# Attention over 32 heads: the sums of the values rotate through one line of four PSUM banks, and their matmuls come in pairs behind every four scores

## The chip, the cores and the metric

The kernel runs on one core of one Trainium2 chip. Its time is the device time of one execution in microseconds (us). A core has a TensorE (PE in the rows; its weight loads are PEld), a VectorE (DVE), a ScalarE (ACT), a GpSimd (POOL) and a SyncE (SP), each with its own instruction stream. They tell each other of progress by semaphores only. PSUM, where TensorE writes, has eight banks of 128 partitions x 512 fp32; this stage of the kernel uses all eight.

## The reference, cut to what matters

Two blocks, each attention or state-space plus feed-forward, behind a LayerNorm with modulation. The change lies in the first attention alone. It has N=2 batches, S=1024 tokens, D=128 and 16 heads of 8 columns, so 32 (batch, head) pairs:

```python
q = (x @ Wq.T).reshape(N, S, H, hd).transpose(0, 2, 1, 3)      # k, v likewise
energy = jnp.einsum('nhqd,nhkd->nhqk', q, k)
attn = jax.nn.softmax(energy / jnp.sqrt(jnp.float32(hd)), axis=3)
out = jnp.einsum('nhql,nhld->nhqd', attn, v)
```

The softmax's maximum is taken off for each query, so the kernel computes every score twice: once to find the row's maximum, once for the exponential.

## The kernel before, in words

**Legs.** The stage is 16 legs (`NLEG`). A leg is four heads and one half (512) of their queries. For one leg the engines do this:

- `pe_max_score`, called "m": 32 matmuls of 512 columns with 48 rows of the array, bf16 (the fp32 numbers are split in three bf16 parts). Two of them fill one pair of the four `max_ps` banks, that is one tile. `ve_max_score` reduces a tile of 1024 to a maximum per query on VectorE, 16 tiles a leg. The first matmul of a tile waits until the tile two before it has been reduced.
- `pe_score`, called "s": 32 matmuls of 512 columns with 51 rows; the last three rows carry the maximum. Each fills one PSUM bank, which `ac_exp` on ScalarE turns into a 128 x 512 piece of `exp_scores`. The 51 rows of a score and the 48 rows of a maximum lie in different halves of the array for neighbours in the order, so the two run side by side.
- `pe_av`, called "v": the values' sum. One call is four matmuls (the records show eight, since fp32 goes in two passes), each on 32 of the 128 columns of the array and all 128 rows, for 256 queries. 16 calls make a leg; all add into one bank. `ac_av_out` on ScalarE then copies that bank to `av_t`, the mark by which legs are counted below.
- `results`: four fp32 transposes of `av_t` into a bank (`pe_out`), copied to `av_tok` by ScalarE; VectorE's reciprocal and POOL's product follow. `max_turn`: one transpose of the leg's maxima (`pe_max_turn`), copied by ScalarE and sent to the rows of `q_rows` by SP.

**Order.** Everything is issued by one loop over 4 * 16 + 1 rounds. The string `ROUNDS[n % 4]` gives the order of the letters m, s and v in a round: 8 m, 8 s, 4 v. The scores of round n are those of leg n // 4, the maxima run 22 tiles ahead, and the values one round behind, so a leg's first value call stands in the second round of the leg. TensorE, ScalarE and VectorE each run their list in this order, and an instruction that waits holds all behind it on its engine. The maxima of the last leg are done some 40 us before the stage ends; from there on the m's of the string issue nothing.

**Banks.** Before the change the scores, the turn of the maxima and the turn of the results share three banks (`score_k`) in strict rotation: the u-th user takes bank u % 3 and waits until the user u - 3 has been read. The values' sum has a bank of its own (`av_ps`). The first value call of a leg therefore waits for `ac_av_out` of the leg before. To give ScalarE time for that, the string of the second round has four pairs "ms" ahead of its first v, behind two that end the round before.

**Memory for the exponentials.** `exp_scores` has four buffers; the first exponential of a group waits for the value calls of the group four before, which were issued long ago in either order.

Of the kernel before, what the change touches and what calls it, by code (L numbers as in the profile page):

```python
# [3 lines left out]

# [2 lines left out]

# [5 lines left out]
F32 = mybir.dt.float32  # L15
# [7 lines left out]
P = 128  # L23
# [6 lines left out]
CH = 512  # L30
# [96 lines left out]
def wait_from(engine, sem, n):  # L127

    if n > 0:
        engine.wait_ge(sem, n)  # L130
# [16 lines left out]
class Kernel:  # L147
# [294 lines left out]
    def attention(self):  # L442
        nc, A, pe, ve, ac, po, sp = self.nc, self.A, self.pe, self.ve, self.ac, self.po, self.sp
        with ExitStack() as scope:
# [21 lines left out]
            back = [sb(f"av_tok{s}", [P, CH]) for s in range(2)]  # L466
            rows_set, v_set = self.sig("rows_set"), self.sig("v_cols_set")
            mps = scope.enter_context(nc.psum_tensor("max_ps", [P, 4, CH], F32))
            eps = scope.enter_context(nc.psum_tensor("score_k", [P, 3, CH], F32))
            avp = scope.enter_context(nc.psum_tensor("av_ps", [P, CH], F32))  # L470

# [57 lines left out]


            NLEG, NU, AHEAD = BH // 2, 16, 22
            read = []

            def score_bank():

                u = len(read)
                return u % 3, read[u - 3] if u > 2 else (exped.sem, 0)

            def head_rows(leg, j):

# [102 lines left out]
            def max_turn(leg):  # L645

                bank, free = score_bank()
                pe_max_turn(leg, bank, free)
                ac_max_turn(leg, bank)
                sp_max_turn(leg)  # L650
                read.append(turn_read.at())

            def results(leg):

                bank, free = score_bank()
                pe_out(leg, bank, free)
                ac_out(leg, bank)
                read.append(res_out.at())

            def divide(leg):  # L660
                ve_recip(leg)
# [27 lines left out]
            def score(e):  # L689
                if e < 32 * NLEG:  # L690
                    bank, free = score_bank()
                    pe_score(e // 32, e % 32, bank, free)
                    ac_exp(e // 32, e % 32, bank)
                    read.append(exped.at())

            def pe_av(leg, kt, half):


                a, quad = 8 * leg + kt, leg // 2
                qs = slice(half * CH // 2, (half + 1) * CH // 2)  # L700
                if kt == half == 0:
                    pe.wait_ge(v_put.sem, 4 * quad + 4)
                    wait_from(pe, av_out.sem, leg)
                pe.wait_ge(exped.sem, 4 * a + 4)
                for j in range(4):
                    mm = pe.matmul(avp[32 * j:32 * j + 32, qs], va[quad % 2][:, j, kt, :], pt[a % 4][:, j, qs],  # L706
                                   start=(kt == half == 0), stop=(kt == TB - 1), skip_group_check=True)
                if half:
                    mm.then_inc(*av_mm.up())

            def ac_av_out(leg):
                ac.wait_ge(av_mm.sem, 8 * leg + 8)
                wait_from(ac, out_mm.sem, leg - 1)
                ac.activation(ot[leg % 2][:], avp[:], ACT.Copy).then_inc(*av_out.up())

            def ve_gate_heads(b, k):
                ve.tensor_tensor(
# [9 lines left out]


            ring = self.ring
            ring.bind([eps[:, k, :] for k in range(3)] + [avp[:]], first=4)  # L730
            self.ac_silu_c(0)
            cols_ps = self.pe_mod_cols(0)
            ac.wait_ge(*self.in_k.at())
# [154 lines left out]
            def ve_first_batch(step):  # L888


                two = range(step % 4 * 2, step % 4 * 2 + 2)
                if step == 0:
                    ve.wait_ge(divided.sem, NLEG // 2)
                    ve.wait_ge(*m_row0)
                if 0 <= step < 4:
                    for k in two:
                        ve_gate_heads(0, k)
                if step == 4:
                    ve_add_heads(0, TB)
                    ve.wait_ge(*gated.at())  # L900
                if 4 <= step < 8:
                    for t in two:
                        self.ve_ln_stat(self.X, t)
                if step == 8:
                    self.ve_ln_aggr(0, TB)
                    roots.append(self.po_ln_root(0, TB))
                if 12 <= step < 16:
                    normed.extend(self.ve_ln_apply(self.X, t, roots[0]) for t in two)
# [17 lines left out]

            ROUNDS = ("msmsvmsmsvvmsmsvmsms", "msmsmsmsvmsmsvvmsmsv", "msmsvmsmsvmsmsvmsmsv", "msmsvmsmsvmsmsvmsmsv")
            normed, roots = [], []  # L930
            for n in range(4 * NLEG + 1):
                leg, place = n // 4, n % 4
                e, v, a = 8 * n, 2 * AHEAD + 8 * n, 4 * n - 4
                for what in ROUNDS[place]:
                    if what == "s":
                        score(e)
                        e += 1
                    elif what == "m":
                        max_score(v)
                        v += 1  # L940
                        if v % 2 == 0:
                            ve_first_batch(v // 2 - NLEG * NU - 1)
                    elif n:
                        pe_av(a // 16, a // 2 % 8, a % 2)
                        if a % 16 == 15:
                            ac_av_out(a // 16)
                        a += 1
                if place == 0 and leg:
                    if leg % 2 == 0 and leg < NLEG:
                        po_put_v(leg // 2)  # L950
                if place == 1 and 0 < leg < NLEG:
                    results(leg - 1)
                if place == 2 and 0 < leg < NLEG:
                    divide(leg - 1)
                    if leg == NLEG - 1:
# [2166 lines left out]
```

## Time and profile before

| | us |
|---|---|
| median of 3 runs (lowest, highest) | 1151.91 (1146.47, 1158.07) |
| the profiled execution | 1158.34 |
| its span, first to last instruction | 1157.0 |
| TensorE busy in the span | 1040.8 (90%) |
| VectorE busy | 974.8 (84%) |
| ScalarE busy | 805.0 (70%) |
| TensorE's mean granted clock | 0.935 |

The attention stage of the change lies between 62 us, when the first exponential starts, and 391 us. In the page's 40 slices of 29 us these are slices 3 to 13. The busy share of TensorE counts matmuls from issue to the modelled end of a record, and neighbours overlap; 99% is therefore no proof that the array is full. In the timeline a matmul's row says when it starts; how fast matmuls can follow one another is read from the distance of starts.

The granted clock is 1.00 at 2.4 GHz and 0.50 at 1.2 GHz.

### The profile page before, as it was taken

To read this page: it belongs to the slowest core of one execution; us is meant where nothing else is said; L and a number is where in the kernel's file an instruction comes from. 1 tells how busy PE (TensorE), PEld (TensorE's weight loads), DVE (VectorE), ACT (ScalarE), POOL (GpSimd) and SP (SyncE) were. 2 spreads that over 40 slices of the span, in tenths; PEclk is the share of its full clock that TensorE was granted. 3 is DMA by queue.
4 is the path that set the end of the run, shared out by engine and by line. 5 is a ranking of instruction groups with operands and counts; after the bars stand their busy time and mean duration, and the time that the engine had idled before them with its cause. 6 is when DMAs were issued, how large, how long until landed. Compare 5 with 4: busy or idle time off the path is not lost. (4 is left out here: it accounts for less than half of the span.)

```text
span 1157.0 us, 21250 instructions
## 1 busy us (share of the span) xinstructions
PE 1040.8 (90%) x7771; PEld 648.1 (56%) x7771; DVE 974.8 (84%) x1319; ACT 805.0 (70%) x1576; POOL 539.3 (47%) x485
## 2 busy tenths in 40 slices
PE   6899999999999887898999999899999994699994
PEld 4222222222222233357998885468888873398883
DVE  6889999999995577879999997889999997787774
ACT  3279988999997553896988862998888832255551
POOL 5400431010101112015988993038999983168884
PEclk9779999999997798889999999899999996699998
DMA  5210100001004330015999990108999976443335
GB/s 156 68 43 15 30 15 19 26 16 30 15 2 74 93 76 16 6 55 123 248 242 230 219 245 6 59 8 193 228 250 231 231 173 241 86 93 64 63 63 135
DMA packets 65608, 121.17 MB, mean 105 GB/s; under 512 B 15598, under 2 KB 33902, under 8 KB 65504
## 3 DMA queue, kind: packets, MB, share of 16 engines
q0 software_dynamic: 19872, 52.79, 24.5%
q1 hardware_dynamic: 43928, 64.82, 18.0%
q10 hardware_dynamic: 1704, 2.20, 0.6%
q8 instruction: 63, 1.03, 0.4%
q14 instruction: 41, 0.34, 0.1%
HBM read 58.02 MB, written 13.32 MB: 62 GB/s over the span
## 5 line engine op out<-in xcount | busy, mean ns | idle before, releaser
L2258 PEld LDWEIGHTS m_pair<-filter_w,delta_x_t 128*128 128x128 f32 x2560 | 294.0, 192 | 42.3 <-issue 42.3
L571 DVE TENSOR_REDUCE neg_max<-max_ps 128x1 f32<-128x1024 f32 x256 | 295.8, 1214 | 16.5 <-PE max_ps L560 16.2
L2258 PE MATMUL m_pair<-filter_w,delta_x_t 128*128 128x112 f32 (+3 forms) x2560 | 298.5, 276 | 9.1 <-DVE h_t L2285 3.3
L687 ACT ACTIVATE exp_scores<-score_k 128x512 f32<-128x512 f32 x512 | 271.1, 606 | 37.0 <-PE score_k L679 31.5
L2234 ACT ACTIVATE decay<-delta,a_log 128x1024 f32<-128x1024 f32 x128 | 145.7, 1142 | 49.2 <-DVE normed L2285 29.2
L560 PE MATMUL max_ps<-k_rows,q_rows 48*128 48x512 bf16 x512 | 163.4, 401 | 12.4 <-DVE neg_max L571 10.7
L679 PE MATMUL score_k<-q_rows,k_rows 51*128 51x512 bf16 x512 | 167.5, 399 | 2.4 <-ACT exp_scores L687 0.6
L2226 ACT ACTIVATE filter_w<-filter,b_t 128x112 f32<-128x112 f32 (+1 forms) x576 | 167.4, 374 | 0.0
L706 PE MATMUL av_ps<-exp_scores,v_cols 128*32 128x256 f32 x2048 | 163.6, 405 | 0.0
L580 POOL CAST neg_max_parts<-neg_max 128x16 bf16<-128x16 f32 x16 | 3.1, 196 | 236.6 <-DVE neg_max L571 236.6
L706 PEld LDWEIGHTS av_ps<-exp_scores,v_cols 128*32 128x32 f32 x2048 | 44.9, 110 | 97.3 <-ACT exp_scores L687 50.0
L560 PEld LDWEIGHTS max_ps<-k_rows,q_rows 48*128 48x128 bf16 x512 | 29.5, 95 | 117.2 <-DVE neg_max L571 75.5
L2276 DVE TENSOR_TENSOR_SCAN m_pair<-decay,m_pair 128x1024 f32<-128x1024 f32 x38 | 87.0, 2290 | 1.6 <-PE m_pair L2258 1.2
L2323 POOL TENSOR_TENSOR h_t<-h_t,c_row 128x1024 f32<-128x1024 f32 x30 | 81.4, 2715 | 12.1 <-DVE h_t L2285 12.1
L2323 POOL TENSOR_TENSOR normed<-normed,c_row 128x1024 f32<-128x1024 f32 x28 | 76.0, 2715 | 23.7 <-DVE normed L2285 23.7
L2285 DVE TENSOR_TENSOR_SCAN normed<-decay,m_pair 128x1024 f32<-128x1024 f32 x32 | 73.0, 2281 | 8.8 <-PE m_pair L2258 8.8
L2285 DVE TENSOR_TENSOR_SCAN h_t<-decay,m_pair 128x1024 f32<-128x1024 f32 x32 | 73.0, 2281 | 6.0 <-PE m_pair L2258 6.0
L2929 PE MATMUL gate_up_ps<-tile_t,gate_up 128*128 128x128 f32 x624 | 76.3, 275 | 0.0
L2929 PEld LDWEIGHTS gate_up_ps<-tile_t,gate_up 128*128 128x128 f32 x624 | 72.6, 192 | 0.0
L2973 POOL DMA_INDIRECT moe_sum<-tile_out,row_to x39 | 62.1, 1592 | 20.5 <-issue 10.7
L2371 PE MATMUL m_pair<-delta_x,ident 128*128 128x512 f32 x136 | 68.3, 598 | 0.0
L2942 ACT ACTIVATE silu_gate<-gate 128x512 f32<-128x512 f32 x39 | 24.6, 631 | 59.1 <-DVE gate L2937 59.1
(330 smaller groups left out, 1611.2 us busy)
## 6 DMA issues: line engine op xcount, KB each, us to landing
c_row<-c_rows SPq DMA_DIRECT2D x64, 512.0 KB, 6.0
x_inner<-normed POOLq DMA_DIRECT2D x16, 512.0 KB, 6.7
delta_x<-mod_memory POOLq DMA_DIRECT2D x15, 512.0 KB, 8.2
delta_x<-x_inner POOLq DMA_DIRECT2D x15, 512.0 KB, 8.2
x_inner<-h_t POOLq DMA_DIRECT2D x14, 512.0 KB, 6.1
mod_memory<-h_t POOLq DMA_DIRECT2D x14, 512.0 KB, 9.3
mod_memory<-normed POOLq DMA_DIRECT2D x12, 512.0 KB, 9.1
gate_up_all<-in_gate_up_w SPq DMA_DIRECT2D x8, 512.0 KB, 7.1
```

The costliest lines, as they stand in the source:

```text
L560: mm = pe.matmul(mps[:, t % 2 * 2 + half, :], qp[row:row + KR, s, leg % 2, qt * P:(qt + 1) * P], kp[row:row + KR, s, half * CH:(half + 1) ...
L571: ve.tensor_reduce(nm[leg % 2][:, 4 * j + qt:4 * j + qt + 1], mps[:, bank:bank + 2, :].rearrange("p a q -> p (a q)"), AX_X, ALU.max, negat ...
L679: pe.matmul(eps[:, bank, :], kp[row:row + KM, s, kt * P:(kt + 1) * P], qp[row:row + KM, s, leg % 2, :], start=True, stop=True).then_inc(*s ...
L687: ac.activation(pt[a % 4][:, HEADS[r % 4], :], eps[:, bank, :], ACT.Exp, scale=SC).then_inc(*exped.up())
L706: mm = pe.matmul(avp[32 * j:32 * j + 32, qs], va[quad % 2][:, j, kt, :], pt[a % 4][:, j, qs], start=(kt == half == 0), stop=(kt == TB - 1) ...
L2226: w = ac.activation(wf[g % 3][:, lo:c * STEP + P], tri[min(c, 1)][:], ACT.Copy, scale=self.bT[b][:, c, n:n + 1])
L2234: ac.activation(da[u % 4], delta[:, blk, b, :], ACT.Exp, scale=am[:, l, blk, n:n + 1]).then_inc(*decay.up())
L2258: mm = pe.matmul(vps[blk][:, lo:hi], self.duT[b][:, c, blk * P:(blk + 1) * P], wf[g % 3][:, lo:hi], start=True, stop=True)
L2276: ve.tensor_tensor_scan(to, da[u % 4], vps[0][:], 0.0, ALU.mult, ALU.add).then_inc(*hs.up())
L2285: ve.tensor_tensor_scan(hh[g % 4], da[u % 4], vps[1][:], 0.0, ALU.mult, ALU.add).then_inc(*hs.up())
L2323: po.tensor_tensor(yacc[b][1] if n == 1 else hh[g % 4], hh[g % 4], csb[g % 3][:], ALU.mult).then_inc(*yg.up())
L2929: mm = pe.matmul(gups[j % 2][:, half, f * P:(f + 1) * P], gu[j % 3][:, half * FF + f * P:half * FF + (f + 1) * P], xt[j % 2][:], start=Tru ...
```

## The change

The private bank of the values goes away. Four banks of `score_k` stand in one line (`idle_banks`): who needs a bank takes the first in the line, and it goes to the end of the line, with the semaphore that tells when it was read. The first value call of a leg takes the first bank of the line and keeps it until `ac_av_out`, so the scores have three banks while a leg's values are summed, as before, and four from the issue of `ac_av_out` to the next leg's first value call.

The strings of `ROUNDS` are new. Every half round is four pairs "ms" and then two v. `results` moves from the end of the second round of a leg to a place inside it (the letter "o", behind its fifth pair).

```diff
-            eps = scope.enter_context(nc.psum_tensor("score_k", [P, 3, CH], F32))
-            avp = scope.enter_context(nc.psum_tensor("av_ps", [P, CH], F32))
+            eps = scope.enter_context(nc.psum_tensor("score_k", [P, 4, CH], F32))
...
-            read = []
+            idle_banks = deque((k, (exped.sem, 0)) for k in range(4))
+            av_bank = {}
             def score_bank():
-                u = len(read)
-                return u % 3, read[u - 3] if u > 2 else (exped.sem, 0)
+                return idle_banks.popleft()
...
-                    read.append(exped.at())
+                    idle_banks.append((bank, exped.at()))
...
                 if kt == half == 0:
+                    av_bank[leg], free = score_bank()
                     pe.wait_ge(v_put.sem, 4 * quad + 4)
-                    wait_from(pe, av_out.sem, leg)
+                    wait_from(pe, *free)
...
-                ac.activation(ot[leg % 2][:], avp[:], ACT.Copy).then_inc(*av_out.up())
+                ac.activation(ot[leg % 2][:], eps[:, av_bank[leg], :], ACT.Copy).then_inc(*av_out.up())
+                idle_banks.append((av_bank[leg], av_out.at()))
...
-            ROUNDS = ("msmsvmsmsvvmsmsvmsms", "msmsmsmsvmsmsvvmsmsv", "msmsvmsmsvmsmsvmsmsv", "msmsvmsmsvmsmsvmsmsv")
+            ROUNDS = ("msmsmsmsvvmsmsmsmsvv", "msmsmsmsvvmsomsmsmsvv", "msmsmsmsvvmsmsmsmsvv", "msmsmsmsvvmsmsmsmsvv")
...
+                    elif what == "o":
+                        if 0 < leg < NLEG:
+                            results(leg - 1)
...
-                if place == 1 and 0 < leg < NLEG:
-                    results(leg - 1)
```

How the list of TensorE changes is seen at three places. The names: L560 (L559 after the change) is m, L679 (L678) is s, L706 is v, L622 (L621) the turn of the results; `exped` counts the exponentials done, `max_read` the reduced tiles.

TensorE in the middle of a leg, before:

```order
L706 MATMUL av_ps<-exp_scores,v_cols 32x256 x3
L560 MATMUL max_ps<-k_rows,q_rows 128x512 [waits max_read]
L679 MATMUL score_k<-q_rows,k_rows 128x512 [waits exped]
L560 MATMUL max_ps<-k_rows,q_rows 128x512
L679 MATMUL score_k<-q_rows,k_rows 128x512 [waits exped]
L706 MATMUL av_ps<-exp_scores,v_cols 32x256 [waits exped]
L706 MATMUL av_ps<-exp_scores,v_cols 32x256 x3
```

and after the change, from one pair of value calls to the next:

```order
L706 MATMUL score_k<-exp_scores,v_cols 32x256 x3
L559 MATMUL max_ps<-k_rows,q_rows 128x512 [waits max_read]
L678 MATMUL score_k<-q_rows,k_rows 128x512 [waits exped]
L559 MATMUL max_ps<-k_rows,q_rows 128x512
L678 MATMUL score_k<-q_rows,k_rows 128x512 [waits exped]
L559 MATMUL max_ps<-k_rows,q_rows 128x512 [waits max_read]
L678 MATMUL score_k<-q_rows,k_rows 128x512 [waits exped]
L559 MATMUL max_ps<-k_rows,q_rows 128x512
L678 MATMUL score_k<-q_rows,k_rows 128x512 [waits exped]
L706 MATMUL score_k<-exp_scores,v_cols 32x256 [waits exped]
L706 MATMUL score_k<-exp_scores,v_cols 32x256 x3
L706 MATMUL score_k<-exp_scores,v_cols 32x256 [waits exped]
```

Between two stretches of value matmuls there stand four scores in place of two, and the stretch is two calls long. A leg has 8 such stretches in place of 14.

TensorE where the values of a new leg begin, before (two more pairs, and the last value call of the old leg, stand ahead of these rows):

```order
L560 MATMUL max_ps<-k_rows,q_rows 128x512
L679 MATMUL score_k<-q_rows,k_rows 128x512 [waits exped]
L560 MATMUL max_ps<-k_rows,q_rows 128x512 [waits max_read]
L679 MATMUL score_k<-q_rows,k_rows 128x512 [waits exped]
L560 MATMUL max_ps<-k_rows,q_rows 128x512
L679 MATMUL score_k<-q_rows,k_rows 128x512 [waits exped]
L706 MATMUL av_ps<-exp_scores,v_cols 32x256 [waits exped,av_out,v_put]
L706 MATMUL av_ps<-exp_scores,v_cols 32x256 x3
```

and after:

```order
L706 MATMUL score_k<-exp_scores,v_cols 32x256 x3
L559 MATMUL max_ps<-k_rows,q_rows 128x512 [waits max_read]
L678 MATMUL score_k<-q_rows,k_rows 128x512 [waits exped]
L559 MATMUL max_ps<-k_rows,q_rows 128x512
L678 MATMUL score_k<-q_rows,k_rows 128x512 [waits exped]
L559 MATMUL max_ps<-k_rows,q_rows 128x512 [waits max_read]
L678 MATMUL score_k<-q_rows,k_rows 128x512 [waits exped]
L559 MATMUL max_ps<-k_rows,q_rows 128x512
L678 MATMUL score_k<-q_rows,k_rows 128x512 [waits av_out]
L706 MATMUL score_k<-exp_scores,v_cols 32x256 [waits exped,v_put]
L706 MATMUL score_k<-exp_scores,v_cols 32x256 x3
```

The six pairs without a value call have become four, as anywhere else. The wait for `av_out` has moved from the value call to the fourth score, which gets the bank of the old sum.

TensorE at the turn of the results, after (before, L622 stood between two stretches, right behind a value call):

```order
L559 MATMUL max_ps<-k_rows,q_rows 128x512 [waits max_read]
L678 MATMUL score_k<-q_rows,k_rows 128x512 [waits exped]
L621 MATMUL score_k<-ident,av_t 128x128 [waits exped,av_out]
L621 MATMUL score_k<-ident,av_t 128x128 x3
L559 MATMUL max_ps<-k_rows,q_rows 128x512
L678 MATMUL score_k<-q_rows,k_rows 128x512 [waits exped]
L559 MATMUL max_ps<-k_rows,q_rows 128x512 [waits max_read]
L678 MATMUL score_k<-q_rows,k_rows 128x512 [waits exped]
L559 MATMUL max_ps<-k_rows,q_rows 128x512
L678 MATMUL score_k<-q_rows,k_rows 128x512 [waits res_out]
L706 MATMUL score_k<-exp_scores,v_cols 32x256 [waits exped]
```

The turn now takes one of the three banks in the midst of four scores: the third waits for the exponential of the first, the fourth for the copy of the results (`res_out`).

## Rows read from the trace of the kernel before

**Rows 1.** Windows of two legs: length, busy PE, PEld, DVE, ACT, POOL, granted clock, DMA, GB/s.

```profile
206.26:225.72 19.46, 19.11 (x201) 5.58 (x197) 18.50 (x18) 17.92 (x36) 1.95 (x9) 1.00 0.07 22
...
166.07:186.76 20.69, 19.18 (x201) 5.57 (x197) 19.64 (x28) 17.92 (x37) 5.29 (x14) 1.00 0.07 21
```

**Rows 2.** The page's costliest groups: operation, count | busy us, mean ns | idle before, releaser.

```profile
L571 DVE TENSOR_REDUCE neg_max<-max_ps 128x1 f32<-128x1024 f32 x256 | 295.8, 1214 | 16.5 <-PE max_ps L560 16.2
...
L687 ACT ACTIVATE exp_scores<-score_k 128x512 f32<-128x512 f32 x512 | 271.1, 606 | 37.0 <-PE score_k L679 31.5
```

**Rows 3.** Timeline of ACT, marks of legs: start us, us, engine, line, out<-in, count.

```profile
86.96 0.60 ACT L714 ACTIVATE av_t<-av_ps 128x512 f32<-128x512 f32 x1
...
361.90 0.60 ACT L714 ACTIVATE av_t<-av_ps 128x512 f32<-128x512 f32 x1
...
389.37 0.60 ACT L714 ACTIVATE av_t<-av_ps 128x512 f32<-128x512 f32 x1 [2.41 <-PE av_ps L706]
```

**Rows 4.** Timeline of PE and ACT between value groups.

```profile
227.85 0.39 PE L679 MATMUL score_k<-q_rows,k_rows 51*128 51x512 bf16 x1
...
228.17 0.64 PE L706 MATMUL av_ps<-exp_scores,v_cols 128*32 128x256 f32 x8
...
229.27 1.07 PE L706 MATMUL av_ps<-exp_scores,v_cols 128*32 128x256 f32 x16
...
230.28 0.39 PE L679 MATMUL score_k<-q_rows,k_rows 51*128 51x512 bf16 x1
...
230.71 1.08 ACT L687 ACTIVATE exp_scores<-score_k 128x512 f32<-128x512 f32 x2 [0.39 <-PE score_k L679]
```

**Rows 5.** Timeline of ACT and PE: an exponential, and the score that waited for it.

```profile
226.20 0.62 ACT L687 ACTIVATE exp_scores<-score_k 128x512 f32<-128x512 f32 x1
...
226.87 0.39 PE L679 MATMUL score_k<-q_rows,k_rows 51*128 51x512 bf16 x1
```

**Rows 6.** Timeline of PE: turns of results and of maxima, each with the next score.

```profile
231.38 0.66 PE L622 MATMUL score_k<-ident,av_t 128*128 128x128 f32 x4
...
231.97 0.39 PE L679 MATMUL score_k<-q_rows,k_rows 51*128 51x512 bf16 x1
...
236.40 0.24 PE L602 MATMUL score_k<-identb,neg_max_parts 128*48 128x128 bf16 x1
...
236.57 0.39 PE L679 MATMUL score_k<-q_rows,k_rows 51*128 51x512 bf16 x1
```

**Rows 7.** Timeline of PE where the last leg's values begin, and its last values.

```profile
360.98 0.64 PE L706 MATMUL av_ps<-exp_scores,v_cols 128*32 128x256 f32 x8
361.55 0.91 PE L679 MATMUL score_k<-q_rows,k_rows 51*128 51x512 bf16 x3
...
364.56 1.08 PE L706 MATMUL av_ps<-exp_scores,v_cols 128*32 128x256 f32 x8
...
386.20 3.10 PE L706 MATMUL av_ps<-exp_scores,v_cols 128*32 128x256 f32 x40
```

**Rows 8.** Windows (columns of rows 1) with the granted clock, end of the stage and first leg.

```profile
358.00:363.80 5.80, 5.10 (x43) 1.37 (x41) 2.14 (x8) 5.21 (x11) 1.47 (x1) 1.00 1.14 210
363.90:387.60 23.70, 23.60 (x130) 5.19 (x133) 5.38 (x26) 13.00 (x25) 1.62 (x3) 0.50 0.21 34
...
62.00:73.70 11.70, 11.14 (x63) 2.31 (x58) 9.23 (x8) 8.48 (x16) 0.00 (x0) 0.50 0.19 57
```

**Rows 9.** Timeline of PE and ACT in the first leg, at the low clock.

```profile
69.91 1.94 PE L706 MATMUL av_ps<-exp_scores,v_cols 128*32 128x256 f32 x16
...
71.78 0.61 PE L679 MATMUL score_k<-q_rows,k_rows 51*128 51x512 bf16 x1
...
72.18 0.63 PE L679 MATMUL score_k<-q_rows,k_rows 51*128 51x512 bf16 x1
...
72.43 1.08 ACT L687 ACTIVATE exp_scores<-score_k 128x512 f32<-128x512 f32 x2 [1.75 <-PE score_k L679]
...
72.74 1.08 PE L706 MATMUL av_ps<-exp_scores,v_cols 128*32 128x256 f32 x8
```

More of the change, by code:

```diff
@@ L7 @@
-from collections import namedtuple
+from collections import deque, namedtuple
 from contextlib import ExitStack
@@ L650, in max_turn @@
                 sp_max_turn(leg)
-                read.append(turn_read.at())
+                idle_banks.append((bank, turn_read.at()))
             def results(leg):
@@ L657, in results @@
                 ac_out(leg, bank)
-                read.append(res_out.at())
+                idle_banks.append((bank, res_out.at()))
             def divide(leg):
@@ L701, in pe_av @@
                 if kt == half == 0:
+                    av_bank[leg], free = score_bank()
                     pe.wait_ge(v_put.sem, 4 * quad + 4)
-                    wait_from(pe, av_out.sem, leg)
+                    wait_from(pe, *free)
                 pe.wait_ge(exped.sem, 4 * a + 4)
                 for j in range(4):
-                    mm = pe.matmul(avp[32 * j:32 * j + 32, qs], va[quad % 2][:, j, kt, :], pt[a % 4][:, j, qs],
+                    mm = pe.matmul(eps[32 * j:32 * j + 32, av_bank[leg], qs], va[quad % 2][:, j, kt, :], pt[a % 4][:, j, qs],
                                    start=(kt == half == 0), stop=(kt == TB - 1), skip_group_check=True)
@@ L729, in attention @@
             ring = self.ring
-            ring.bind([eps[:, k, :] for k in range(3)] + [avp[:]], first=4)
+            ring.bind([eps[:, k, :] for k in range(4)], first=4)
             self.ac_silu_c(0)
```

## The prediction

> **What bounds the stage now.** I first read the windows of whole legs [rows 1]. A leg in mid stage takes 19.46 us. VectorE is busy in 18.50 of them and ScalarE in 17.92, so both are nearly full and neither is quite the bound. In the page's groups VectorE's 16.5 us of idle time ahead of the reductions is almost all put down to TensorE, and so are 31.5 us of ScalarE's ahead of the exponentials [rows 2]: TensorE's list, in which one waiting instruction holds all others, deals the time out. The marks of the legs [rows 3] give 361.90 - 86.96 = 274.94 us for 14 legs. Twelve of 19.46 and two of 20.69 make 274.9; the two long ones carry 1.14 us more of VectorE's work [rows 1]. The last leg, which has no maxima left and so should be shorter, took 27.47 us.
>
> Why it did is in the windows with the clock [rows 8]. Up to 363.8 us the granted clock is 1.00, from 363.9 to 387.6 it is 0.50, the 1.2 GHz level. The timeline [rows 7] shows what TensorE did before it fell: a value call at 360.98, then six lone scores, three of them late behind ScalarE, and the next value call only at 364.56. It rose again at the end, where the last value calls stand back to back [rows 7]. The change moves both things, the mid leg and the last leg, and in opposite directions.
>
> **Mid leg, the time of a half round after the change.** It is four pairs "ms" and two value calls. Three banks are left to the scores while a leg's values are summed, so the fourth score waits until the exponential of the first is done. This gives a closed chain, and every link of it has a row:
>
> - first score to the start of its exponential: 230.28 to 230.71, 0.43 us [rows 4];
> - the exponential: 0.60 [rows 2];
> - its end to the score that waits for the bank: 226.82 to 226.87, 0.05 [rows 5];
> - the fourth score to the first value call: 227.85 to 228.17, 0.32 [rows 4];
> - a pair of value calls to the next first score: 229.27 to 230.28, 1.01 [rows 4].
>
> The sum is 2.41 us. VectorE needs 18.50 / 8 = 2.31 for its two tiles of it and hides under this; the first matmul of the second tile starts before the fourth score and waits for nothing longer. Before the change the same bank count did little harm: only two scores stood between value calls, so the third bank's exponential ran under the values.
>
> Three of a leg's eight half rounds are others. With the turn of the results in it, the fourth score waits for that turn's copy. The turn starts 0.32 behind the first score, its records last 0.66 [rows 6], and then come 0.05, a copy of 0.60 and 0.05: 1.68 in place of 0.43 + 0.60 + 0.05 = 1.08, so 3.0. The turn of the maxima adds 236.40 to 236.57, 0.17 [rows 6]: 2.6. At the change of leg the fourth score waits for `av_t`: the pair's 1.07 [rows 4], 0.05, 0.60 and 0.05, then 0.32, which is 2.1; the first exponential queues behind `av_t`, so I take 2.25. A leg is 5 x 2.41 + 3.0 + 2.6 + 2.25 = 19.9 us, **0.44 more than before**. Its lower bound is VectorE's 18.5; above it I allow 20.2, if the reductions come late as well. The two long legs I leave at 20.7: VectorE's extra work has 19.9 - 18.5 = 1.4 of slack to hide in, but the maxima wait for it in the same list. Sum for the mid stage: 12 x 0.44 = **+5.3 us** (bounds -13 and +10).
>
> What the change takes away on TensorE does not show in this: a value stretch costs 0.32 less the 0.21 that 512 columns take at 2.4 GHz on the way in, and 1.01 less two calls of 0.43 (1.07 - 0.64, or 0.43, from the two forms in [rows 4]) on the way out, 0.26 together. Six stretches fewer are 1.5 us of TensorE a leg. They fall into the wait of the fourth score. The Trainium skill, "TensorEngine Tiling (Array Packing)", Key Properties, says that changing the tiling mode drains the engine. The rows agree that a change costs time, and by this rule alone each leg would get shorter by the drains saved.
>
> **Last leg.** From `av_t` of leg 14 there are six half rounds with scores: 2.25, 3.0 and four of 2.41, or 14.9. Two pairs of value calls follow, 0.86 each, so 16.6 us at the full clock against 27.47: **-10.8 us**. It needs the clock to stay up. The reason to think so: no stretch between value calls is now longer than four scores, where the clock fell behind six; and in mid leg, with the same spacing as in the second half of the stage, the trace has 1.00 throughout [rows 1]. If the clock falls nevertheless, the gain is near 1 (below). The bounds are -11 and 0.
>
> **First leg.** Until 73.7 us the clock is 0.50 [rows 8], in both kernels. Values begin at the same place. I take 0, with bounds of -1.5 (the clock rises a little earlier, since a pair stands at the very start) and +3 (later).
>
> **Other edits.** Ahead of the stage the banks of the projections rotate as before, the same four under other names: 0. On the other engines VectorE's, POOL's and SP's lists are unchanged, and ScalarE issues the same instructions with the results' copy a few places earlier: its work of 17.92 a leg stays under 19.9. The reciprocal and the product get their input earlier, and nobody waits for them in mid stage. The first value call no longer waits for `av_t`; the fourth score ahead of it does, already counted.
>
> **Sum.** On the profiled execution, 1158.34 + 5.3 - 10.8 = 1152.8. That execution lies 6.4 above the median shown, 1151.91. The lowest run, 1146.47, is 11.9 below it, about what a low-clock last leg costs; if some runs before keep the clock there, the median already holds part of my gain, while the cost in mid leg stays. Against the median the two terms nearly cancel. I predict **1153 us**, with 1148 to 1158 as this case's own range. About 1% (11.5 us) is what a measurement of this kernel tells from no change: below 1140.4 is faster, above 1163.4 slower.
>
> **Rivals.**
>
> - *The last leg runs at the low clock all the same.* At 1.2 GHz a half round is 71.78 to 72.43, 0.65, then 0.60 and 0.05, 72.18 to 72.74, 0.56, and 69.91 to 71.78, 1.87 [rows 9]: 3.7 us. The last leg is then 6 x 3.7 + 0.6 + 0.3 for its two odd ones and 2 x 1.73, some 26.5, and the total 1158.34 + 5.3 - 1.0 = 1162.6. For it: the scores fill less than half the rows of the array, and TensorE waits for a bank in every half round. Against it: the shorter stretches without values. Chance 0.15.
> - *The drains were the bound.* If the fourth score's wait is hidden, VectorE sets the leg: 18.5. Then 14 legs save 0.96 each, 13.4, and with the last leg the total is 1158.34 - 13.4 - 10.8 = 1134. For it: TensorE is named for VectorE's idle time, and it has 1.5 us less to do. Against it: the chain of 2.41, none of whose links the change shortens. By the rule of the Trainium skill's page "TensorEngine Tiling (Array Packing)" on drains this would be the time. Chance 0.10.
> - *The clock falls or stays down elsewhere, and it is slower.* The place is the first leg. The clock rose at 73.7 behind value calls that stood close [rows 9]; if the even order with its wait on the fourth score does not bring it up, a leg costs 8 x 3.7 + 1 = 30.6 in place of 19.9. One leg more at the low clock makes 1153 + 10.7 = 1163.7, which is the point from which it decides; with the last leg low as well it is 1173. Against it: each leg of before kept 1.00 once it had it, through six pairs without values. The Trainium skill, "TensorE: Matmul & The Clock Gate", A second HAM failure mode, reports a kernel whose clock swung because TensorE idled briefly between groups as it cycled through PSUM banks; the trace has such waits in each leg at a steady 1.00, so it speaks against the rule so far. Chance 0.08.
> - *The order does not matter*, as the three score banks were not waited for and the clock is a matter of luck: 1152. Chance 0.07, and it falls within my range.
>
> My forecast has 0.60. **Faster** gets 0.13: the drains, and a little of the forecast where median runs keep the clock better than I think. **Slower** gets 0.13: the clock, and that part of the low last leg that ends above 1163.4. **Same** gets 0.74. The range of 1141 to 1164 takes in the low last leg and part of the way to the faster case; outside lie most of the drains' case and the clock's.
>
> **What would show it.** Marks of `av_t` 19.9 us apart in mid stage, value calls in pairs 2.4 us apart with one gap of 3.0 and one of 2.6 a leg, each pair behind a score that waited for ScalarE; VectorE idle 1.4 us a leg, not 0.96. The last leg at 1.00 and near 16.6 us. Marks 18.5 apart would refute the chain. A last leg above 25 us with a clock of 0.50 would refute the second term.

## The result, and the profile after

The changed kernel takes 1161.04 us (median of 11 runs, 1156.13 to 1163.76) against 1148.35 us of the kernel before (11 runs beside it, 1143.78 to 1158.07). The ratio is 1.0102 with a 95% interval of 1.0075 to 1.0129: 1% slower. The forecast was 1153 with a range of 1141 to 1164 and most of the chance on "within 1%"; the time lies in the range, 8.0 us above the forecast, and the ratio just beyond the 1% that parted "same" from "slower" there. Ratios leave out executions far above the rest (one of 1854.45 us with single value calls and the line, one of 1947.98 us of the kernel before); the medians and counts given below have them in. The profiled execution of the changed kernel took 1158.43 us, almost the same as the 1158.34 of the profile before. That agreement is the sum of two large differences, and another execution of the kernel before lacks most of the second (the last experiment).

The windows of the changed kernel answer to those of before [rows 1, 8]. The columns are the same: a mid leg, one of the two long legs, the last leg, and the 14 legs from the first to the fifteenth `av_t`.

```profile
231.41:251.66 20.25, 19.92 (x199) 6.55 (x197) 18.94 (x18) 17.80 (x36) 1.24 (x5) 1.00 0.08 21
127.42:149.03 21.61, 19.68 (x199) 6.47 (x197) 20.20 (x28) 17.90 (x36) 4.05 (x12) 1.00 0.06 20
373.18:390.03 16.85, 14.24 (x157) 5.91 (x156) 5.39 (x26) 13.40 (x26) 1.62 (x3) 1.00 0.32 52
86.90:373.18 286.28, 276.08 (x2739) 91.36 (x2736) 264.08 (x282) 249.42 (x491) 44.60 (x124) 1.00 0.08 22
```

A mid leg is 20.25 us, 0.8 longer; a long leg 21.61, 0.9 longer; 14 legs are 286.28 in place of 274.94, **11.3 us longer**. The last leg is 16.85 at a clock of 1.00, where it was 27.47 [rows 3, 8]: **10.6 us shorter**. The first `av_t` stands at 86.90, before at 86.96, and from the last one to the end of the span it is 767.1 us, before 767.6. With these two small differences the two large ones add up to the 0.1 us that lie between the profiles.

The page's groups of the stage:

```profile
L686 ACT ACTIVATE exp_scores<-score_k 128x512 f32<-128x512 f32 x512 | 266.1, 604 | 43.6 <-PE score_k L678 39.8
...
L678 PE MATMUL score_k<-q_rows,k_rows 51*128 51x512 bf16 x512 | 169.2, 391 | 6.3 <-ACT exp_scores L686 4.6
```

and the scores' row in that of before:

```profile
L679 PE MATMUL score_k<-q_rows,k_rows 51*128 51x512 bf16 x512 | 167.5, 399 | 2.4 <-ACT exp_scores L687 0.6
```

ScalarE's wait for scores has grown from 31.5 [rows 2] to 39.8 us, and that of the scores on TensorE for ScalarE from 0.6 to 4.6. In the view of waits of two legs (211 to 252 us) the loads of the scores' weights wait 5.2 us for the exponentials, where two legs of before (206 to 245 us) have 2.3:

```profile
PEld score_k L678 <- ACT exp_scores L686: 5.2, 12, 0.5
...
ACT exp_scores L686 <- PE score_k L678: 4.0, 10, 0.4
```

The loop shows in the timeline of TensorE from one pair of value calls to the next (every row of the score L678 and of the pair L706, the maxima left out):

```profile
246.60 0.39 PE L678 MATMUL score_k<-q_rows,k_rows 51*128 51x512 bf16 x1
...
246.83 0.38 PE L678 MATMUL score_k<-q_rows,k_rows 51*128 51x512 bf16 x1
...
247.19 0.39 PE L678 MATMUL score_k<-q_rows,k_rows 51*128 51x512 bf16 x1
...
247.74 0.39 PE L678 MATMUL score_k<-q_rows,k_rows 51*128 51x512 bf16 x1
248.06 1.07 PE L706 MATMUL score_k<-exp_scores,v_cols 128*32 128x256 f32 x16
...
249.07 0.39 PE L678 MATMUL score_k<-q_rows,k_rows 51*128 51x512 bf16 x1
```

and in that of ScalarE, the same stretch and the next leg's beginning:

```profile
247.09 2.06 ACT L686 ACTIVATE exp_scores<-score_k 128x512 f32<-128x512 f32 x4 [0.40 <-PE score_k L678]
249.55 2.07 ACT L686 ACTIVATE exp_scores<-score_k 128x512 f32<-128x512 f32 x4 [0.40 <-PE score_k L678]
251.66 0.60 ACT L714 ACTIVATE av_t<-score_k 128x512 f32<-128x512 f32 x1
252.15 2.78 ACT L686 ACTIVATE exp_scores<-score_k 128x512 f32<-128x512 f32 x5
254.86 0.60 ACT L628 ACTIVATE av_tok<-score_k 128x512 f32<-128x512 f32 x1
```

The first score starts at 246.60 and its exponential at 247.09, which ends 0.60 later; the fourth score starts at 247.74, 0.05 behind that end. (The third starts together with the maxima's matmul ahead of it, which waits for a reduction; the fourth comes later still, so this wait does not decide.) Then come the pair at 248.06 and the next first score at 249.07. ScalarE does four exponentials in 2.06 us and then is idle for 0.40, each time until the first score behind the pair.

### The profile page after: what moved, and what is told of

Same layout as the page of the kernel before. It is cut to its first block and busy times, and to the rows that moved or that the text cites. A ratio compares the mean times of both kernels' runs of the same rounds, so it can differ in the third digit from the quotient of the medians.

```text
span 1157.1 us, 21250 instructions
## 1 busy us (share of the span) xinstructions
PE 1039.2 (90%) x7771; PEld 661.5 (57%) x7771; DVE 979.9 (85%) x1319; ACT 802.6 (69%) x1576; POOL 538.8 (47%) x485
## 5 line engine op out<-in xcount | busy, mean ns | idle before, releaser
L570 DVE TENSOR_REDUCE neg_max<-max_ps 128x1 f32<-128x1024 f32 x256 | 300.5, 1220 | 21.6 <-PE max_ps L559 15.6
L686 ACT ACTIVATE exp_scores<-score_k 128x512 f32<-128x512 f32 x512 | 266.1, 604 | 43.6 <-PE score_k L678 39.8
L2236 ACT ACTIVATE decay<-delta,a_log 128x1024 f32<-128x1024 f32 x128 | 145.7, 1141 | 47.9 <-DVE normed L2287 27.9
L678 PE MATMUL score_k<-q_rows,k_rows 51*128 51x512 bf16 x512 | 169.2, 391 | 6.3 <-ACT exp_scores L686 4.6
L559 PE MATMUL max_ps<-k_rows,q_rows 48*128 48x512 bf16 x512 | 161.4, 403 | 10.4 <-DVE neg_max L570 7.5
L706 PE MATMUL score_k<-exp_scores,v_cols 128*32 128x256 f32 x2048 | 137.8, 387 | 1.6
L559 PEld LDWEIGHTS max_ps<-k_rows,q_rows 48*128 48x128 bf16 x512 | 30.5, 96 | 121.4 <-DVE neg_max L570 85.5
L706 PEld LDWEIGHTS score_k<-exp_scores,v_cols 128*32 128x32 f32 x2048 | 55.1, 109 | 54.6 <-issue 31.6
L678 PEld LDWEIGHTS score_k<-q_rows,k_rows 51*128 51x128 bf16 x512 | 38.7, 94 | 60.3 <-ACT exp_scores L686 47.8
L2975 POOL DMA_INDIRECT moe_sum<-tile_out,row_to x39 | 62.0, 1589 | 20.8 <-DVE tile_out L2965 10.5
```

What stands on the lines that cost most here:

```text
L559: mm = pe.matmul(mps[:, t % 2 * 2 + half, :], qp[row:row + KR, s, leg % 2, qt * P:(qt + 1) * P], kp[row:row + KR, s, half * CH:(half + 1) ...
L570: ve.tensor_reduce(nm[leg % 2][:, 4 * j + qt:4 * j + qt + 1], mps[:, bank:bank + 2, :].rearrange("p a q -> p (a q)"), AX_X, ALU.max, negat ...
L678: pe.matmul(eps[:, bank, :], kp[row:row + KM, s, kt * P:(kt + 1) * P], qp[row:row + KM, s, leg % 2, :], start=True, stop=True).then_inc(*s ...
L686: ac.activation(pt[a % 4][:, HEADS[r % 4], :], eps[:, bank, :], ACT.Exp, scale=SC).then_inc(*exped.up())
L706: mm = pe.matmul(eps[32 * j:32 * j + 32, av_bank[leg], qs], va[quad % 2][:, j, kt, :], pt[a % 4][:, j, qs], start=(kt == half == 0), stop= ...
L2236: ac.activation(da[u % 4], delta[:, blk, b, :], ACT.Exp, scale=am[:, l, blk, n:n + 1]).then_inc(*decay.up())
```

## The experiments

Each was profiled and timed against the kernel before. I name them by what they are; "leg" is the distance of two marks of `av_t` in mid stage, read from windows as above.

**The line of banks alone**, the order of before:

```diff
-            ROUNDS = ("msmsmsmsvvmsmsmsmsvv", "msmsmsmsvvmsomsmsmsvv", ...
+            ROUNDS = ("msmsvmsmsvvmsmsvmsms", "msmsmsmsvmsmsvvmsmsv", "msmsvmsmsvmsmsvmsmsv", "msmsvmsmsvmsmsvmsmsv")
...
-                    elif what == "o":
-                        if 0 < leg < NLEG:
-                            results(leg - 1)
...
+                if place == 1 and 0 < leg < NLEG:
+                    results(leg - 1)
```

> The one line of four banks alone, with the order of before (14 stretches of value calls a leg, the turn of the results at the end of the second round). Theory A (the time of a leg is the chain first score, exponential, fourth score, pair of value calls, so the order is what costs): the marks of av_t stay near 19.4 us apart, 1147 to 1149 us in all, ratio 0.998 to 1.003 to before. Theory B (the line costs, since scores now queue behind av_t's copy and the results): marks near 20.2, ratio near 1.01. The six lone scores of the last leg are still there, so its clock can fall to 0.50 as before.

```profile
225.23:244.56 19.33, 18.60 (x201) 5.53 (x197) 18.50 (x18) 17.85 (x37) 1.24 (x5) 1.00 0.08 22
...
360.51:378.88 18.37, 17.91 (x159) 5.52 (x158) 5.39 (x26) 14.55 (x29) 1.62 (x3) 0.91 0.43 64
```

The legs are 19.33 us, 0.13 shorter than before. The line is a small gain and not the loss. The ratio was 1.0056 (1.0022 to 1.0091) all the same, above the 1.003 that I had as the upper end, since the runs fall in two groups: five at 1145 to 1149, with a mean granted clock of 0.939 to 0.941, and five at 1156 to 1159, with 0.925 to 0.932. None of the upper group was profiled. In the profiled one, of the lower group, the clock was at 0.50 for a short while only, and the last leg took 18.37:

```profile
364.00:367.30 3.30, 3.30 (x27) 0.86 (x26) 0.00 (x0) 1.89 (x5) 0.00 (x0) 0.50 1.00 153
```

**The pairs alone**, with the private bank (the change's ROUNDS and its "o" in the kernel before):

> The new order (pairs of value calls behind four scores, results inside the second round) with the values' private bank and three rotating banks as before. Theory A: marks at least as far apart as in the changed kernel, 20.3 to 20.7 us, since the first value call of a leg now waits for av_t as well; ratio to before 1.010 to 1.016. Theory B (the line costs): marks near 19.5, ratio near 1.00.

```profile
232.88:253.41 20.53, 20.24 (x199) 6.48 (x197) 18.94 (x18) 17.81 (x35) 1.25 (x5) 1.00 0.08 21
```

20.53 us a leg, 1165.57 us, ratio 1.0171 (1.0127 to 1.0215). The order is the whole of the loss, and the line gives 0.27 a leg of it back. (The order is two things here, the pairs and the turn of the results inside a round; no run parts them.)

**Single value calls behind every two scores**, with the line:

```diff
-            ROUNDS = ("msmsmsmsvvmsmsmsmsvv", ...
+            ROUNDS = ("msmsvmsmsvmsmsvmsmsv",) * 4
...
-                    elif what == "o":
-                        if 0 < leg < NLEG:
-                            results(leg - 1)
...
+                if place == 1 and 0 < leg < NLEG:
+                    results(leg - 1)
```

> The line of four banks kept, but every round is four times (four m/s letters, one value call): single value calls behind every two scores, 16 stretches a leg. Theory A: the fourth score no longer follows the first one before a value stretch, so TensorE's wait for ScalarE hides under the value call and VectorE sets the leg: marks 18.7 to 19.0 us apart although TensorE changes tiling twice as often; about 0.6 us less than before on 14 legs, and the last leg near 15.6 us at clock 1.00: 1138 to 1143 us, ratio 0.990 to 0.994. Theory C (changes between value calls and scores are what TensorE pays for): two stretches a leg more than before cost 0.26 us each, marks near 20.0, ratio 1.005 to 1.01.

```profile
221.54:240.20 18.66, 18.66 (x201) 5.26 (x197) 18.32 (x18) 17.95 (x36) 1.24 (x5) 1.00 0.08 23
122.20:143.81 21.61, 20.01 (x199) 5.38 (x197) 20.41 (x28) 18.10 (x36) 4.98 (x13) 0.92 0.07 20
352.12:367.64 15.52, 15.52 (x157) 4.97 (x156) 5.39 (x26) 13.59 (x27) 1.62 (x3) 1.00 0.47 67
```

18.66 us a leg. 1137.49 us, ratio 0.9915 (0.9880 to 0.9950), faster than either kernel, with 16 stretches of value calls a leg, the most of all orders. Theory C, by which the changes between value calls and scores are what TensorE pays for, had asked for marks near 20.0; it falls as the account of the changed kernel.

What bounds this leg is not what I expected. VectorE is busy in 18.32 us of it and waits for TensorE once, for 0.34. TensorE's records leave no gap, and in the timeline its list runs at its own pace:

```profile
226.61 0.38 PE L678 MATMUL score_k<-q_rows,k_rows 51*128 51x512 bf16 x1
226.92 0.64 PE L706 MATMUL score_k<-exp_scores,v_cols 128*32 128x256 f32 x8
...
227.49 0.39 PE L678 MATMUL score_k<-q_rows,k_rows 51*128 51x512 bf16 x1
...
227.72 0.38 PE L678 MATMUL score_k<-q_rows,k_rows 51*128 51x512 bf16 x1
```

The distances of 0.31, 0.57 and 0.23 us make 1.11 for each stretch, 16 times a leg, and the two turns, at 0.59 and 0.24, and one wait of 0.13 fill the rest of the 18.66. So TensorE is full here and VectorE nearly so. With the 0.26 us a stretch that the prediction worked out, 16 switches are some 4.2 us of TensorE's list (an estimate); what they would give back in this order was not tried. The long legs did not gain: 21.61 us, with a mean clock of 0.92 in that window.

**The same order with the private bank:**

> The same even single value calls with the private bank and three rotating banks of before. Theory A: the first value call of a leg waits for av_t once, some 0.3 us a leg more than with the line: marks near 19.1, ratio 0.993 to 0.998. If the line has no part in it: marks as in the run with the line, 18.8.

19.00 us a leg, 1142.48 us, ratio 0.9959 (0.9932 to 0.9987). The line is worth 0.34 a leg here.

**Half an exponential** in the changed kernel; from the fifth group on, half of `exp_scores` keeps old values:

```diff
-                ac.activation(pt[a % 4][:, HEADS[r % 4], :], eps[:, bank, :], ACT.Exp, scale=SC).then_inc(*exped.up())
+                cols = slice(0, CH if a < 4 else CH // 2)
+                ac.activation(pt[a % 4][:, HEADS[r % 4], cols], eps[:, bank, cols], ACT.Exp, scale=SC).then_inc(*exped.up())
```

> The changed kernel, but from the fifth group of scores on the exponential covers only 256 of the 512 columns (the rest of exp_scores keeps old values): one link of the chain gets 0.2 us shorter. Theory A: a half round falls from 2.46 to about 2.3 us, where VectorE takes over, and marks from 20.26 to about 19.3. Theory D (the long stretch of two value calls starves VectorE's reductions): nothing of it changes, marks stay at 20.26.

```profile
226.73:245.92 19.19, 18.22 (x199) 6.43 (x197) 18.58 (x18) 11.66 (x35) 1.24 (x5) 1.00 0.08 22
124.55:145.96 21.41, 18.68 (x199) 6.37 (x197) 20.49 (x28) 11.67 (x36) 4.80 (x13) 0.98 0.07 20
```

19.19 us a leg: 1.06 less for a link 0.2 shorter, eight times a leg and less where VectorE steps in. 1146.69 us, ratio 0.9972 (0.9943 to 1.0002). ScalarE's throughput can't be meant, since it was idle in each half round before; its latency is.

**Half a reduction** in the changed kernel (the maximum is taken over half of the scores):

```diff
-                                 mps[:, bank:bank + 2, :].rearrange("p a q -> p (a q)"), AX_X, ALU.max,
+                                 mps[:, bank, :], AX_X, ALU.max,
```

> The changed kernel with VectorE's reductions over 512 of the 1024 scores of a tile, half their time. Theory A: marks stay at 20.26 us except in the two legs with VectorE's extra work (21.6), which fall to 20.3. Theory D (VectorE starved): marks fall by 0.5 us or more.

```profile
222.58:242.83 20.25, 19.48 (x199) 7.15 (x197) 10.47 (x17) 17.81 (x35) 1.24 (x5) 1.00 0.07 21
121.31:141.57 20.26, 19.48 (x199) 7.16 (x197) 11.95 (x27) 17.81 (x36) 3.09 (x11) 1.00 0.07 21
```

VectorE falls from 18.9 to 10.5 us a leg and the leg stays at 20.25. The long legs fall to the same 20.26, so what makes them long is VectorE. 1150.85 us in all, ratio 1.0017 (0.9986 to 1.0048): I had not said where the total would go. The first `av_t` comes 6.1 us earlier (80.81 against 86.90). Ahead of it there is a stretch with maxima alone, and the clock rises some 7 us earlier too (from 66 us on it is 1.00, in the changed kernel from 72 on); the two are not parted. The long legs give 2.7. Theory D, that VectorE's reductions are starved, falls for the mid legs.

**ScalarE's second wait moved** in the changed kernel:

```diff
-                if r % 4 == 0:
-                    wait_from(ac, av_mm.sem, a - 3)
+                if r % 4 == 3:
+                    wait_from(ac, av_mm.sem, a - 2)
```

> The changed kernel; ScalarE's wait for the value calls of the group four before stands ahead of the last exponential of the group before, no longer ahead of the first of the group. In the trace the exponentials with both waits start 0.10 us behind the score's record, those with one wait 0.04. If the second wait costs that, a half round falls from 2.46 to 2.41 us, marks from 20.26 to 19.9, 5 us in all. If the 0.10 belongs to the place behind a value stretch, nothing changes.

Timelines of ScalarE and of TensorE:

```profile
241.92 2.06 ACT L686 ACTIVATE exp_scores<-score_k 128x512 f32<-128x512 f32 x4 [0.34 <-PE score_k L678]
```

```profile
241.49 0.39 PE L678 MATMUL score_k<-q_rows,k_rows 51*128 51x512 bf16 x1
...
243.90 0.39 PE L678 MATMUL score_k<-q_rows,k_rows 51*128 51x512 bf16 x1
```

The score at 241.49 has its exponential at 241.92, 0.43 later in place of 0.49, and the next first score comes 2.41 behind. The leg is 19.89, the ratio 1.0046 (1.0025 to 1.0067), the median 1155.65: 5.4 less than the changed kernel against other runs of before. In the order of single calls the same edit does nothing for the leg:

> Single value calls behind every two scores, the line of four banks, and ScalarE's wait for the value calls moved ahead of the last exponential of the group before. Theory A: mid legs are VectorE's there (18.66 us against 18.3 of reductions one behind the other), so 0.06 us less in ScalarE's start hides: marks 18.6 to 18.7, ratio 0.990 to 0.993, same as without the move. If the second wait still costs 0.06 in each group, marks fall to 18.4 or below.

18.66 us again, 1137.56 us, ratio 0.9890 (0.9852 to 0.9929).

**The kernel before with another order in its last leg alone:**

```diff
-                for what in ROUNDS[place]:
+                for what in (ROUNDS[place] if leg < NLEG - 1 else "msmsvmsmsvmsmsvmsmsv"):
```

> The kernel before with the order of its last leg alone changed to a single value call behind every two scores. Theory E (the six scores without a value call bring the clock down in the last leg of some executions, and that is the 27.47 us of the profile of before): the last leg takes 15.5 to 17 us at clock 1.00 in every execution, the highest runs of before (1152 to 1158) vanish, median 1144 to 1148, ratio 0.994 to 0.999. Theory F (the clock falls there because the maxima have ended, whatever the order): last leg at times above 25 us at clock 0.50, and the same spread of times as before.

```profile
225.28:244.74 19.46, 19.11 (x201) 5.58 (x197) 18.51 (x18) 17.93 (x37) 1.24 (x5) 1.00 0.08 22
...
362.05:377.91 15.86, 15.47 (x157) 4.86 (x156) 5.38 (x26) 13.74 (x27) 1.62 (x3) 1.00 0.46 66
```

The last leg takes 15.86 us at 1.00. The times go from 1142.76 to 1151.02 over 12 runs, where before shows 1143.99 to 1161.69 over 35; 13 of them above 1151.02; median 1146.28, ratio 0.9964 (0.9943 to 0.9986). The distance ahead of the last leg is 20.03 in place of 19.42, since the first scores of the new order stand in it.

**The changed kernel with the order of before in its last leg alone:**

```diff
+                OLD = ("msmsvmsmsvvmsmsvmsms", "msmsmsmsvmsmsvvmsmsvo", "msmsvmsmsvmsmsvmsmsv", "msmsvmsmsvmsmsvmsmsv")
-                for what in ROUNDS[place]:
+                for what in (ROUNDS[place] if leg < NLEG - 1 else OLD[place]):
```

> The changed kernel, but the last leg alone has the order of before with its six scores without a value call. Theory E (these six scores are what lets the clock fall in the last leg, in executions where they fall on the wrong moment): the times split in two groups some 9 to 11 us apart, as they did with the line alone (1145 to 1148 and 1156 to 1158), the upper near 1170; where the profile shows the fall, the last leg is above 18 us and the clock 0.50 behind the six scores. Theory F (the clock in the last leg does not depend on the order): one group of 1156 to 1164 as with the changed kernel, last leg near 17 us.

Windows up to the six lone scores, behind them, and the last leg:

```profile
368.40:375.40 7.00, 6.54 (x54) 1.80 (x52) 2.14 (x8) 6.26 (x13) 0.48 (x1) 1.00 1.17 196
375.60:399.30 23.70, 23.70 (x139) 5.82 (x142) 5.39 (x26) 11.53 (x22) 1.62 (x3) 0.50 0.14 21
```

```profile
372.24:399.81 27.57, 27.11 (x159) 6.72 (x158) 5.39 (x26) 14.89 (x30) 1.62 (x3) 0.57 0.26 39
```

The clock fell in the last leg, 1.3 us behind the six scores and with one value call between, where in the kernel before it fell while they ran; the last leg took 27.57 us. I had expected the two groups 9 to 11 us apart, and they lie 11 to 15. The four times are 1157.04 and 1159.76, 1170.81 and 1171.98; the ratio was 1.0106 (1.0042 to 1.0171). In this profile the clock fell in a long leg as well, which took 22.39 at a mean clock of 0.96; just ahead TensorE had waited 1.07 us for a reduction (to 144.99) and 0.53 for an exponential (to 146.12). The changed kernel, whose list is the same up to there, has the same two waits at 146.22 and 147.35, and its clock stayed at 1.00.

**The kernel before, profiled again:**

> The kernel before, unchanged, profiled once more. Theory E: mid legs 19.46 us as before; the last leg is either near 17 us with the clock at 1.00 or well above 20 us with the clock at 0.50 from behind the six scores, by the execution. Theory F: above 25 us at 0.50 again.

```profile
225.30:244.76 19.46, 19.11 (x201) 5.58 (x197) 18.50 (x18) 17.92 (x36) 1.24 (x5) 1.00 0.08 22
...
361.48:381.23 19.75, 19.05 (x159) 5.49 (x158) 5.39 (x26) 14.66 (x29) 1.62 (x3) 0.83 0.39 59
```

```profile
363.20:369.90 6.70, 6.70 (x38) 1.37 (x38) 0.00 (x0) 4.00 (x8) 0.00 (x0) 0.50 0.82 123
370.10:381.20 11.10, 11.10 (x117) 3.68 (x117) 5.39 (x26) 8.94 (x17) 1.62 (x3) 1.00 0.01 3
```

The same 19.46 us a leg, but the clock fell for 6.8 us only and the last leg took 19.75, 7.7 less than in the profile that the prediction was read from. I had expected either near 17 us at 1.00 or well above 20; it lay between.

## Why the prediction was right, and where it was off

**The chain.** The mechanism is shown: shortening a link of it shortens the leg (half an exponential, the moved wait), halving VectorE's work does not in a mid leg, and taking the pairs away, and with them the turn's place inside a round, brings 20.26 to 18.66. Its links by the trace after are 0.49, 0.60, 0.05, 0.32 and 1.01, or 2.47, where I had 2.41 [rows 2, 4, 5]. **The link that was mis-sized is the first.** I took 0.43 from the exponential at 230.71 [rows 4], the third of its group of four. The one that matters is the first of a group, which has a second wait (for the value calls of the group four before); it starts 0.10 behind the score's record, the third 0.04. Moving that wait took out just this. The odd half rounds were 2.99, 2.63 and 2.32 us, from the starts of the pairs:

```profile
250.52 1.07 PE L706 MATMUL score_k<-exp_scores,v_cols 128*32 128x256 f32 x16
...
252.84 1.07 PE L706 MATMUL score_k<-exp_scores,v_cols 128*32 128x256 f32 x16
...
255.83 1.07 PE L706 MATMUL score_k<-exp_scores,v_cols 128*32 128x256 f32 x16
...
258.30 1.07 PE L706 MATMUL score_k<-exp_scores,v_cols 128*32 128x256 f32 x16
...
260.76 1.07 PE L706 MATMUL score_k<-exp_scores,v_cols 128*32 128x256 f32 x16
...
263.39 1.07 PE L706 MATMUL score_k<-exp_scores,v_cols 128*32 128x256 f32 x16
```

against 3.0, 2.6 and 2.25. In all a leg is 20.26 and not 19.9, so twelve legs cost 9.6 and not 5.3. That is above the 20.2 I allowed, and with the long legs the stage's 11.3 is above the bound of +10.

**The long legs** I left at 20.7; they went to 21.6, 1.8 us for both. The slack of 1.4 us that I had VectorE's extra work hide in was no slack: behind VectorE's small extra instructions a reduction comes late and holds the maxima at the head of TensorE's list (1.07 us at 146.22), and the chain waits behind them. Half a reduction brought these legs to 20.26.

**The drains.** The rival that had them as the bound of this change is refuted: fewer switches and a longer leg, more switches and a shorter one. The Trainium skill, "TensorEngine Tiling (Array Packing)", Key Properties, says that a change of mode drains the engine. The trace agrees that a change costs time, 0.26 us for the way in and out; what that time consists of it does not show. Taking six away gave nothing here, where TensorE has to wait anyway. With single value calls it does not wait, and there they may count.

**The last leg.** 16.85 against a forecast of 16.6, at a clock of 1.00, as the step said. The order with the six lone scores is shown to be what brings the fall: all four profiles that have it in the last leg show it (the kernel before twice, the line alone, and the changed kernel with the old last leg at 27.57), and none of the nine with another order there does. That it is the six scores, and not another part of that order, is argued from the place of the fall: while the six run in the two profiles of the kernel before, 1.3 and 1.4 us behind their end in the other two.

**The base of the sum is what failed here.** The profile before was an execution in which the clock stayed down for 24 us. Another profile of the same kernel has 19.75, and the median of 1148.35 lies 10 below the first profile. Taking the fall away from the kernel before gained 3.0 us at the median (1149.32 to 1146.28). I had seen this and written that the median may already hold part of the gain, but still held the forecast to 1153. With 19.75 as the last leg of before, the gain is 2.9 and not 10.8, and 1148.35 + 11.3 - 2.9 makes 1156.8. The measured median is 1161.04. The last 4.2 us are not accounted for: the profiled execution of the changed kernel, at 1158.43, lies below its own median, and no execution near that median was profiled.

**Luck.** The mechanisms of both terms were right, but the first came out at twice its size and most of the second was missing at the median. That the time still fell in the range was in part luck: the range went up to 1164 for a last leg at the low clock, which did not occur, and the errors of the sum used that room.

**The first leg and other edits** at zero: right in the sum, 86.90 against 86.96. It hides two differences. The first exponential starts at 60.91 in place of 62.05, and the clock is up from 72 us on in place of 74; the first leg from there is 1.1 longer. No run says whether the early start comes of the change.

**Slower by the clock:** that rival did not come about; the changed kernel reached its first `av_t` at the same time as before, and its windows from there to the end of the last leg have 1.00. It ended slower for another reason, the size of the chain's term and the missing gain.

What stays open: how often the clock falls in the last leg of the kernel before and for how long, and whether such a fall is what parts the two groups of the line alone. Also open are the falls in long legs: both long legs of the three kernels with single value calls and of half an exponential, and one of the changed kernel with the old last leg. With single calls TensorE had been idle for 1.60 us just ahead, waiting for a late reduction; spreading VectorE's extra work was not tried.

## What to carry to other kernels

Where a few banks rotate between a producer and a consumer, an order with more uses between two long stretches of other work than there are banks (four on three here) makes the producer wait out the consumer's whole latency with nothing beside it; two uses on three banks did not. In such a loop neither engine's busy time tells the bound. Fewer switches are worth nothing if they lengthen that loop: here 16 switches a leg beat 8 by 1.6 us of 20. And before a term as large as a thirtieth of a stage is booked as a gain, look whether the profiled execution stands for the median: one that lies 6 us above it may hold just that term.

## What the runs showed of the hardware

- A ScalarE instruction that has two semaphores to wait for starts 0.10 us behind the record of the matmul that releases it (246.60 + 0.39 to 247.09); with one, 0.04 (241.49 + 0.39 to 241.92, with the wait moved). The other semaphore counts value calls issued long before.
- TensorE's clock fell from 1.00 to 0.50 in the last leg although TensorE's longest idle time just ahead was 0.59 us, as its timeline in the kernel before shows between two halves of the six lone scores:

```profile
363.05 1.58 PE L679 MATMUL score_k<-q_rows,k_rows 51*128 51x512 bf16 x3 [0.59 <-ACT exp_scores L687]
```

  With the line alone and in the changed kernel with the old last leg the six followed one another without idle time, 2.38 us for all, and it fell too. What stood ahead of the fall were these six 512-column matmuls of 51 rows without one of the full array among them; in those two runs one value call and two more scores stood behind them. The same six with the maxima's matmuls beside them left it at 1.00 in every mid leg. It was low for 3.3 us in one window, 6.7 and 23.7 in others.
- It fell behind short waits too, but not each time. The Trainium skill, "TensorE: Matmul & The Clock Gate", A second HAM failure mode, tells of a kernel whose clock swung with brief waits for PSUM banks. The changed kernel waits for one in each half round, and its windows from 86.9 to 390 us have 1.00. With the same list up to its last leg, another execution had the clock fall behind waits of 1.07 and 0.53 us in a long leg. So here the page's case is seen in one execution and not in the other.
- At the low clock the last leg's work costs 27.5 us in place of the 15.9 and 16.9 that other orders took at 1.00. In the low stretch of 23.7 us TensorE's records leave no gap, while ScalarE is busy in 11.53 us and VectorE in 5.39.
